# Strip network of the last stage: up products over 256 columns in place of two halves of 128

## Chip, cores and metric

The kernel runs on one core of a Trainium2 chip. The metric is the device time of the whole kernel in microseconds; less is better. The kernel before was run three times.

## What is computed

The input x has 16 sequences of 256 tokens and 256 features, float32. Four layers follow one another, each added to x: an attention layer, a gated cumulative layer, a mixture of experts with a shared network, and a recurrent network. Cut to the parts that the last stage of the kernel computes:

```python
# layer 3, the shared network of the mixture (256 -> 1024 -> 256)
shared = jax.nn.gelu(context_c @ sw1 + sb1, approximate=True) @ sw2 + sb2
return out + shared            # out: the routed experts

# layer 4, the recurrence
xw = jnp.einsum('ntd,dh->nth', x, Wx) + b
def step(prev_h, xw_t):
    next_h = jnp.tanh(xw_t + prev_h @ Wh)
    return (next_h, next_h)
_, hs = jax.lax.scan(step, h0, jnp.swapaxes(xw, 0, 1))
```

The recurrence has 256 steps that can only be done one after the other. The shared network has no such order, but its result for a token must be there before the recurrence reaches that token.

## The kernel before, in words

Three stages run one after the other: attention and the gated layer, the routed experts, and the last stage, `shared_and_rnn` (line 1635). Only the last one is touched. It begins at about 955 us of the span.

The last stage does the shared network and the recurrence at the same time. Tokens are taken in chunks of 16 (CH), so that a chunk has N = 16 sequences x 16 tokens = 256 columns; there are 16 chunks, and the first two were done by the stage before, so 14 are left. Features lie on the 128 partitions in two groups (DC = 2). The hidden 1024 of the shared network are FC = 8 blocks of 128.

*Strips.* Every product of this stage is cut into four matmuls whose results are 32 partitions high (QD = 4, QW = 32), one for each quarter of the output partitions; the helper `strips` (lines 1730 to 1734) issues the four for a product of the shared network. They use the array's column groups beside one another. A float32 matmul leaves two matmul and two weight-load records in the trace, so a strip product of four matmuls has 8 of each.

*Recurrence.* For each step k, `recur(k)` on TensorE (line 1711) multiplies the state with Wh: 8 matmuls of 64 columns (16 records, line 1716) into the PSUM tile `pr`. VectorE transposes the result (line 1813), ScalarE takes the tanh (line 1789), and the state is ready for step k+1. For each pair of steps, `drive` (line 1719) adds the input product with Wx (line 1727, 16 records) after an even step. VectorE puts the bias back after an odd step (line 1816).

*Shared network between the steps.* `ffn(c)` (line 1736) is a generator that yields after each strip product. For a block n of the hidden units of a chunk, it waits until the gelu has freed the PSUM tile (a ring of three) and issues the up products: two halves of the 256 columns, and for each half the two feature groups, so four strip products of 128 columns. The last one signals `up_ok`. ScalarE then takes the gelu of the whole 256 columns (line 1797) and signals `gelu_ok`. Two blocks later come the down products, two strip products of 256 columns, which sum over the eight blocks in `pys` and signal `down_ok`. When a chunk is complete, VectorE adds it to x (line 1827) for the recurrence, which needs the tile that POOL has staged for the output before (line 1859). POOL also joins the two parts of x into `xf` for the next chunks (line 1852) and waits for `up_ok` before it overwrites a tile.

*The order of the work* is written by hand. `order()` (line 1677) lists the strip products with a size in units, 1 for an up product of 128 columns and 2 for a down product of 256; `quota(k)` (line 1673) grants a step 4 units, or 3 in every fourth step from step 64 on:

```python
return 3 if k >= 4 * CH and k % 4 == 2 else 4
```

A loop (lines 1688 to 1695) turns this into `counts[k]`, the number of strip products that TensorE issues after the recurrence's own matmuls of step k, and into `ended`, the step in which a block ends. What is taken too much from one quota is missing in the next. From `ended` come the steps in which ScalarE has its gelus (after the tanh of that step, line 1794) and VectorE its adds (line 1837). With a quota of 4, a step holds for example four up products, or two down products, or two up and one down. The last down product falls into step 234; the remaining steps have only the recurrence.

Of the kernel before, what the change touches and what calls it, by code (L numbers as in the profile page):

```python
# [12 lines left out]
P = 128  # L13
B, T, D = 16, 256, 256
DC = D // P
# [1280 lines left out]
def experts(nc, env):  # L1296
# [9 lines left out]
    with st:  # L1306
# [24 lines left out]
        with ExitStack() as routed:  # L1331
# [225 lines left out]
            def _(pe):  # L1557
# [68 lines left out]
                for t in range(TICKS + 2):  # L1626
                    if t < TICKS:
                        up(t)
                    if t >= 2:
                        down(t - 2)  # L1630

        shared_and_rnn(nc, env, locals())


def shared_and_rnn(nc, env, ex):
# [4 lines left out]
    xhi, xlo, raw1, raw2, wx, wh = (ex[k] for k in ("xhi", "xlo", "raw1", "raw2", "wx_sb", "wh_sb"))  # L1640
    N = B * CH
    QD = 4
    QW = P // QD
    RING = 3
    PAIRS = T // 2
    HALF = N // 2
    KEEP = 4
    st = ExitStack()
    with st:  # L1649
# [6 lines left out]
        xf = sb(st, "xf", [P, 2, DC, B, CH])  # L1656
        ph = [ps(st, f"phs{q}", [P, 512]) for q in range(RING)]
# [7 lines left out]
        xf_ready, up_ok, gelu_ok, down_ok = (sem(st, n) for n in ("xf_ready", "up_ok", "gelu_ok", "down_ok"))  # L1665
# [3 lines left out]
        def quad(w, j):  # L1669

            return w.rearrange("p (k q) -> p k q", q=P)[:, :, QW * j:QW * (j + 1)]
# [5 lines left out]
        def order():  # L1677

            for c in range(FIRST, NCH):
                for n in range(FC + 2):  # L1680
                    if n < FC:
                        for a in range(2 * DC):
                            yield 1, (("up", c, n) if a == 2 * DC - 1 else None)
                    if n >= 2:
                        for m in range(DC):
                            yield 2, (("down", c, n - 2) if m == DC - 1 else None)

        counts, ended, left, item = [0] * T, {}, 0, order()
        for k in range(T):
            left += quota(k)  # L1690
# [17 lines left out]
        @block.tensor  # L1708
        def _(pe):
            def recur(k):  # L1710
                pe.wait_ge(h_ready, k + 1)
                prev = hs[:, (k - 1) // CH % 2, (k - 1) % CH]
                dst = steps[k // 2 % 2].rearrange("p (k q) -> p k q", q=QW)
                for c in range(DC):
                    for j in range(QD):
                        i = nc.tensor.matmul(dst[QW * j:QW * (j + 1)], prev[:, c], quad(wh[:, c], j), start=False, stop=(c == DC - 1), skip_group_check=True)  # L1716
                i.then_inc(step_done, 1)

            def drive(p):

                c, s, at = 2 * p // CH, 2 * p // CH % 2, 2 * p % CH
                pe.wait_ge(x_ready, c + 1)
                dst = steps[p % 2].rearrange("p (k q) -> p k q", q=QW)
                pe.wait_ge(bias_set, p + 1)
                for k in range(DC):
                    for j in range(QD):
                        nc.tensor.matmul(dst[QW * j:QW * (j + 1)], xc[:, s, k, at:at + 2].rearrange("p t b -> p (t b)"), quad(wx[:, k], j),  # L1727
                                         start=False, stop=False, skip_group_check=True)

            def strips(dst, weights, moving, start, stop):  # L1730

                for j in range(QD):
                    i = nc.tensor.matmul(dst[QW * j:QW * (j + 1)], weights[:, QW * j:QW * (j + 1)], moving, start=start, stop=stop)  # L1733
                return i

            def ffn(c):

                pe.wait_ge(xf_ready, c - FIRST + 1)
                for n in range(FC + 2):
                    if n < FC:  # L1740
                        pe.wait_ge(gelu_ok, FC * (c - FIRST) + n + 1)
                        for a in (0, HALF):
                            for k in range(DC):
                                moving = xf[:, c % 2, k].rearrange("p b t -> p (b t)")[:, a:a + HALF]
                                i = strips(ph[n % RING][:, a:a + HALF], raw1[:, k, n * P:(n + 1) * P], moving, k == 0, k == DC - 1)
                                if k == DC - 1 and a > 0:
                                    i.then_inc(up_ok, 1)
                                yield
                    if n >= 2:
                        f = n - 2  # L1750
                        pe.wait_ge(gelu_ok, FC * (c - FIRST) + f + RING + 1)
                        if f == 0 and c > FIRST:
                            pe.wait_ge(x_ready, c)
                        for m in range(DC):
                            i = strips(py[:, m, 0:N], raw2[:, f, m * P:(m + 1) * P], g[:, f % KEEP], f == 0, f == FC - 1)
                            if m == DC - 1:
                                i.then_inc(down_ok, 1)
                            yield

            def all_ffn():  # L1760
                for c in range(FIRST, NCH):
                    yield from ffn(c)

            pe.wait_ge(ex["wxh_in"], 32)
            work = all_ffn()
            pe.wait_ge(row1_set, 2)
            for half_pair in steps:
                dst = half_pair.rearrange("p (k q) -> p k q", q=QW)
                for j in range(QD):
                    i = nc.tensor.matmul(dst[QW * j:QW * (j + 1)], row1[:], quad(vec("rnn_b_row"), j), start=True, stop=True, skip_group_check=True)  # L1770
                i.then_inc(bias_rows, 1)
            drive(0)
            for k in range(T):
                recur(k)
                if k % 2 == 0 and k // 2 + 1 < PAIRS:
                    drive(k // 2 + 1)
                for _ in range(counts[k]):
                    next(work, None)
# [157 lines left out]
```

## Time and profile before

| what | us |
|---|---|
| median of 3 runs | 1312.1 |
| lowest, highest | 1312.03, 1315.19 |
| the profiled execution, its own time | 1311.1 |
| span of that execution, first to last instruction | 1309.3 |
| TensorE matmuls busy in the span | 1198.6 (92%) |
| TensorE weight loads busy in the span | 946.4 (72%) |
| VectorE, ScalarE, POOL busy | 805.0, 622.5, 335.7 |
| mean granted clock of TensorE | 0.973 of full |

Times of the trace count from the first instruction. PE stands for TensorE's matmuls, PEld for its weight loads (they overlap the matmuls), DVE for VectorE, ACT for ScalarE. Matmuls are pipelined and their ends are modelled: a record's duration is longer than the time until the next one can start, so many records of some 270 ns follow one another every 27 ns. "issue" as what an engine waited for means that the profile shows nothing that it waited for. Some matmul records can be missing.

### The profile page before, as it was taken

What the parts mean: (1) busy time and instruction counts of PE and PEld (TensorE: products, weight loads), DVE (VectorE), ACT (ScalarE), POOL (GpSimd) and SP (SyncE); (2) the same over time, 40 slices, a digit from 0 to 9 for tenths busy, and PEclk for the clock granted to TensorE, in tenths of its full rate; (3) what the DMA queues carried; (4) which work ended last, traced back from release to release, by engine and by line L of the source; (5) the groups of instructions that cost most, each with busy time, mean ns of one, the idle gap of its engine ahead of it and who ended that gap; (6) DMA issues with size and microseconds to landing.
All of it is one profiled execution on the core that took longest, in us unless ns stands there. A gap on an engine that the chain in (4) does not pass through costs nothing. (4 is left out here: it accounts for less than half of the span.)

```text
span 1309.3 us, 42133 instructions
## 1 busy us (share of the span) xinstructions
PE 1198.6 (92%) x18136; PEld 946.4 (72%) x18136; DVE 805.0 (61%) x1823; ACT 622.5 (48%) x1168; POOL 335.7 (26%) x311
## 2 busy tenths in 40 slices
PE   4699999999999888499999999999989989999995
PEld 2466666767665443159999999999977777777773
DVE  6887887878875979956666665666632332323322
ACT  2377777777767879333333333333323333333331
POOL 1446445544452679600000000000020101111100
PEclk9799999999999989799999999999999999999995
DMA  9013221212212100059999999999600000000000
GB/s 358 2 51 98 68 81 50 99 50 73 76 50 82 65 0 1 0 212 396 379 366 366 360 368 370 359 369 363 224 12 13 13 20 13 21 13 21 21 13 19
DMA packets 77096, 180.41 MB, mean 138 GB/s; under 512 B 3824, under 2 KB 14192, under 8 KB 76656
## 3 DMA queue, kind: packets, MB, share of 16 engines
q1 hardware_dynamic: 76912, 177.72, 37.6%
q8 instruction: 144, 2.36, 0.8%
q14 instruction: 40, 0.33, 0.1%
HBM read 156.47 MB, written 20.97 MB: 136 GB/s over the span
## 5 line engine op out<-in xcount | busy, mean ns | idle before, releaser
L1416 ACT ACTIVATE g<-ph,b 128x256 f32<-128x256 f32 x256 | 121.6, 475 | 247.9 <-PE ph L1605 247.8
L1813 DVE STREAM_TRANSPOSE preT<-pr 128x64 f32<-128x64 f32 x256 | 64.0, 250 | 234.7 <-PE pr L1716 234.0
L693 DVE TENSOR_REDUCE mx<-pR 128x4 f32<-128x1024 f32 x128 | 156.4, 1225 | 65.0 <-PE pR L899 63.6
L1525 DVE CAST ghi<-g 128x256 fp32r<-128x256 f32 x256 | 74.8, 292 | 128.2 <-ACT g L1416 128.0
L1733 PE MATMUL phs<-xf,raw 128*32 128x128 f32 x3584 | 144.0, 275 | 10.5 <-issue 10.4
L1789 ACT ACTIVATE hs<-preT 128x32 f32<-128x32 f32 x256 | 58.7, 229 | 197.7 <-DVE preT L1813 196.0
L1621 PE MATMUL py<-ghi,w 128*128 128x256 f32 x512 | 145.7, 285 | 1.7 <-DVE glo L1527 1.6
L1603 PE MATMUL ph<-xhi,w 128*128 128x256 f32 x512 | 145.3, 284 | 0.0
L1604 PE MATMUL ph<-xlo,w 128*128 128x256 f32 x512 | 144.9, 283 | 0.0
L1622 PE MATMUL py<-glo,w 128*128 128x256 f32 x512 | 144.9, 283 | 0.0
L1623 PE MATMUL py<-ghi,w 128*128 128x256 f32 x512 | 144.9, 283 | 0.0
L1605 PE MATMUL ph<-xhi,w 128*128 128x256 f32 x512 | 144.9, 283 | 0.0
L1716 PE MATMUL pr<-wh_sb,hs 128*32 128x64 f32 x4096 | 130.7, 228 | 15.0 <-ACT hs L1789 9.2
L1733 PE MATMUL pys<-gs,raw 128*32 128x256 f32 x1792 | 136.8, 380 | 2.4 <-issue 1.3
L490 ACT ACTIVATE raw<-pR 128x1024 f32<-128x1024 f32 x128 | 129.3, 1024 | 18.8 <-PE pR L908 17.2
L1716 PEld LDWEIGHTS pr<-wh_sb,hs 128*32 128x32 f32 x4096 | 99.8, 113 | 48.2 <-ACT hs L1789 34.2
L1733 PEld LDWEIGHTS phs<-xf,raw 128*32 128x32 f32 x3584 | 106.9, 111 | 19.4 <-issue 17.2
L1527 DVE TENSOR_TENSOR glo<-g,ghi 128x256 fp32r<-128x256 f32 x256 | 108.9, 426 | 8.8
L1842 POOL MEMSET row<- 128x32 f32 x1 | 0.1, 125 | 404.6 <-POOLq L1331 404.6
L1621 PEld LDWEIGHTS py<-ghi,w 128*128 128x128 f32 x512 | 98.2, 192 | 3.2 <-DVE glo L1527 3.1
L1604 PEld LDWEIGHTS ph<-xlo,w 128*128 128x128 f32 x512 | 98.3, 192 | 0.2 <-issue 0.2
L1603 PEld LDWEIGHTS ph<-xhi,w 128*128 128x128 f32 x512 | 98.3, 192 | 0.2 <-issue 0.2
(219 smaller groups left out, 2461.2 us busy)
## 6 DMA issues: line engine op xcount, KB each, us to landing
w<-weight_halves SPq DMA_DIRECT2D x128, 1024.0 KB, 8.0
weight_halves<-wparts SPq DMA_DIRECT2D x32, 512.0 KB, 4.0
modw<-in_ew SPq DMA_DIRECT2D x32, 256.0 KB, 4.7
xn<-in_x_tok SPq DMA_DIRECT2D x4, 1024.0 KB, 11.8
XT<-in_x_dm SPq DMA_DIRECT2D x2, 2048.0 KB, 14.4
out_dm<-staged SPq DMA_DIRECT2D x16, 256.0 KB, 2.4
raw<-in_sw SPq DMA_DIRECT2D x2, 1024.0 KB, 7.5
modw<-in_mod_w SPq DMA_DIRECT2D x1, 768.0 KB, 7.1
```

The costliest lines, as they stand in the source:

```text
L490: nc.scalar.activation(probs[:, j % 4], pR[k][:], ACT.Exp, scale=HD ** -0.5).then_inc(free[k], 1)
L693: nc.vector.reduce_max(mx[:, :, 2 * j:2 * j + 2].rearrange("p t s -> p s t"), pR[k][:].rearrange("p s (t k) -> p s t k", t=TC), AX.X).then ...
L1416: nc.scalar.activation(g[:, t % RING], ph[t % RING][:, 0:T], ACT.Gelu_apprx_tanh, bias=b1[:, n, f:f + 1]).then_inc(gelu_done, 1)
L1527: nc.vector.tensor_tensor(glo[:, t % RING], g[:, t % RING], ghi[:, t % RING].bitcast(fp32), ALU.subtract).then_inc(lo_done, 1)
L1603: nc.tensor.matmul(dst, whi, hi, start=(k == 0), stop=False)
L1604: nc.tensor.matmul(dst, whi, lo, start=False, stop=False)
L1605: i = nc.tensor.matmul(dst, wlo, hi, start=False, stop=(k == DC - 1))
L1621: nc.tensor.matmul(dst, whi, hi, start=(f == 0), stop=False)
L1622: nc.tensor.matmul(dst, whi, lo, start=False, stop=False)
L1623: i = nc.tensor.matmul(dst, wlo, hi, start=False, stop=(f == FC - 1))
L1716: i = nc.tensor.matmul(dst[QW * j:QW * (j + 1)], prev[:, c], quad(wh[:, c], j), start=False, stop=(c == DC - 1), skip_group_check=True)
L1733: i = nc.tensor.matmul(dst[QW * j:QW * (j + 1)], weights[:, QW * j:QW * (j + 1)], moving, start=start, stop=stop)
```

## The change

In `order()` an up product has the size 2, and there are two of them (one for each feature group) in place of four of size 1. In `ffn` the loop over the two halves is gone: each strip product streams all 256 columns, and the last of the two signals `up_ok`. Results, tiles, semaphores and their counts stay.

```diff
@@ -1643,7 +1643,6 @@
     QW = P // QD
     RING = 3
     PAIRS = T // 2
-    HALF = N // 2
     KEEP = 4
@@ -1679,8 +1678,8 @@
             for c in range(FIRST, NCH):
                 for n in range(FC + 2):
                     if n < FC:
-                        for a in range(2 * DC):
-                            yield 1, (("up", c, n) if a == 2 * DC - 1 else None)
+                        for k in range(DC):
+                            yield 2, (("up", c, n) if k == DC - 1 else None)
                     if n >= 2:
                         for m in range(DC):
                             yield 2, (("down", c, n - 2) if m == DC - 1 else None)
@@ -1739,13 +1738,11 @@
                 for n in range(FC + 2):
                     if n < FC:
                         pe.wait_ge(gelu_ok, FC * (c - FIRST) + n + 1)
-                        for a in (0, HALF):
-                            for k in range(DC):
-                                moving = xf[:, c % 2, k].rearrange("p b t -> p (b t)")[:, a:a + HALF]
-                                i = strips(ph[n % RING][:, a:a + HALF], raw1[:, k, n * P:(n + 1) * P], moving, k == 0, k == DC - 1)
-                                if k == DC - 1 and a > 0:
-                                    i.then_inc(up_ok, 1)
-                                yield
+                        for k in range(DC):
+                            i = strips(ph[n % RING][:, 0:N], raw1[:, k, n * P:(n + 1) * P], xf[:, c % 2, k], k == 0, k == DC - 1)
+                            if k == DC - 1:
+                                i.then_inc(up_ok, 1)
+                            yield
                     if n >= 2:
                         f = n - 2
                         pe.wait_ge(gelu_ok, FC * (c - FIRST) + f + RING + 1)
```

## Rows read from the trace of the kernel before

**Rows 1.** Windows of the last stage: length, each engine busy (instructions), clock, DMA share, GB/s

```profile
core 0: us, PE busy (x) PEld busy (x) DVE busy (x) ACT busy (x) POOL busy (x), PEclk, DMA share, GB/s
955.00:1279.80 324.80, 301.39 (x11056) 250.66 (x11056) 99.69 (x384) 104.56 (x348) 37.94 (x43) 0.99 0.05 16
1279.80:1304.10 24.30, 15.67 (x464) 11.27 (x464) 7.52 (x29) 4.35 (x19) 1.41 (x2) 0.57 0.04 13
```

**Rows 2.** Groups by shape, TensorE's matmuls, 955 to 1279.8 us

```profile
line engine op names shapes xcount | busy us, mean ns | idle before us <-releasers
L1733 PE MATMUL phs<-xf,raw 128*32 128x128 f32 x3584 | 144.0, 275 | 10.5 <-issue 10.4
L1733 PE MATMUL pys<-gs,raw 128*32 128x256 f32 x1792 | 136.8, 380 | 2.4 <-issue 1.3 <-ACT gs L1797 0.7
L1716 PE MATMUL pr<-wh_sb,hs 128*32 128x64 f32 x3776 | 118.3, 222 | 5.8 <-issue 4.8
L1727 PE MATMUL pr<-wx_sb,xc 128*32 128x64 f32 x1904 | 57.7, 221 | 4.8 <-issue 3.8 <-DVE pr L1809 0.8
```

**Rows 3.** Chain of work, 1098 to 1106 us: start, us, what

```profile
1099.11 0.44 PE phs L1733 x16
1099.55 0.43 PE pys L1733 x8
1099.98 0.22 PE pr L1716 x16
1100.20 0.22 PE pr L1727 x16
1100.43 0.43 PE pys L1733 x8
1100.86 0.71 issue
```

**Rows 4.** Waits, 955 to 1279.8 us: us in total, times, longest

```profile
engine line waited for: us in total, times, longest us
...
PEld phs L1733 <- issue: 17.2, 23, 1.2
...
PEld pr L1716 <- issue: 8.5, 20, 1.0
PEld pr L1727 <- issue: 5.9, 12, 1.0
PEld pys L1733 <- issue: 5.0, 10, 1.0
```

**Rows 5.** Windows between two pauses (two), and one without a pause; columns as in rows 1

```profile
1072.13:1076.12 3.99, 3.29 (x127) 2.93 (x127) 1.21 (x5) 1.45 (x5) 0.00 (x0) 1.00 0.02 4
1101.56:1105.40 3.84, 3.27 (x127) 2.56 (x128) 1.21 (x5) 1.09 (x4) 0.00 (x0) 1.00 0.02 4
1231.19:1234.38 3.19, 3.19 (x138) 2.94 (x130) 1.80 (x6) 1.39 (x5) 0.00 (x0) 1.00 0.02 5
```

**Rows 6.** Queue of instruction packets (packets, MB, share): 955 to 1279.8, then 1060 to 1105 us

```profile
q8 instruction: 87, 1.43, 1.9%
...
q8 instruction: 12, 0.20, 2.0%
```

**Rows 7.** VectorE in order of time, from two stretches

```profile
978.91 0.25 DVE L1813 STREAM_TRANSPOSE preT<-pr 128x64 f32<-128x64 f32 x1 [0.57 <-PE pr L1716]
979.94 0.61 DVE L1827 TENSOR_TENSOR xc<-XT,pys 128x256 f32<-128x256 f32 x1 [0.78 <-POOL staged L1859]
980.40 0.21 DVE L1813 STREAM_TRANSPOSE preT<-pr 128x64 f32<-128x64 f32 x1
...
1021.96 0.25 DVE L1813 STREAM_TRANSPOSE preT<-pr 128x64 f32<-128x64 f32 x1 [0.57 <-PE pr L1716]
1023.27 0.25 DVE L1813 STREAM_TRANSPOSE preT<-pr 128x64 f32<-128x64 f32 x1 [1.06 <-PE pr L1716]
...
1024.36 0.25 DVE L1813 STREAM_TRANSPOSE preT<-pr 128x64 f32<-128x64 f32 x1 [0.57 <-PE pr L1716]
```

**Rows 8.** All engines in order of time, 1126 to 1132 us

```profile
1127.99 0.43 PE L1716 MATMUL pr<-wh_sb,hs 128*32 128x64 f32 x16
...
1128.77 0.23 ACT L1789 ACTIVATE hs<-preT 128x32 f32<-128x32 f32 x1 [0.83 <-DVE preT L1813]
...
1129.21 0.64 PE L1733 MATMUL pys<-gs,raw 128*32 128x256 f32 x8
...
1129.48 0.47 ACT L1797 ACTIVATE gs<-phs,small 128x256 f32<-128x256 f32 x1 [0.48 <-PE phs L1733]
```

## Prediction

> **What bounds the kernel now.** I read first the windows of the last stage [rows 1]. Everything before 955 us is untouched by the edit. From 955.0 to 1279.8 us the recurrence and the strip network share TensorE; from there to the end only recurrence is left, at a lower clock. The first stretch is 324.8 us and the only one that can change. TensorE is busy in 301.4 of it, at a clock of 0.99 of full (the 2.4 GHz level). So the stretch looks bound by TensorE's work; the question is whether this busy time is columns or something that goes with the number of instructions.
>
> The groups by shape [rows 2] give the counts: 3584 matmul records of the up products (each float32 matmul leaves two records, each with its own weight load), 1792 of the down products, 3776 of the recurrence's state product and 1904 of its input product: 11056, and as many weight loads.
>
> Then the chain of waits of one stretch, which gives the price of a piece when nothing disturbs it [rows 3]: 16 records of up with 128 columns take 0.44 us, 8 records of down with 256 columns 0.43 us, a state product or an input product (16 records of 64 columns) 0.22 us. These are the same 27 ns per record of 128 columns, 54 ns per record of 256 and 14 ns per record of 64: **time follows columns, not instructions**. By this view alone the edit is worth nothing, since 8 records of 256 columns replace 16 of 128. But the last row of the group is 0.71 us of "issue": TensorE had work, all its operands, and did not start.
>
> The waits put down to issue [rows 4] are 65 pauses of the weight-load side, 36.6 us together. Where are they? I cut the stretch from the end of one such pause to the end of the next [rows 5]: 127 matmuls and 127 or 128 weight loads, in 3.99 and in 3.84 us. That is 256 instructions with a semaphore instruction or two, each time, whatever the instructions are. The DMA view shows what comes in such a rhythm [rows 6]: 12 instruction packets in 45 us, 87 in the stretch, 16 KB each by the queue's bytes, against 22112 / 256 = 86.4 blocks of 256 instructions. So TensorE's instructions are fetched one block at a time, and **when the engine has run through a block before the next has come, it stands**. The stretch averages 324.8 / 86.4 = 3.76 us a block. A fetch cycle costs at most 3.19 us where no pause is seen (last of rows 5, 268 instructions) and 3.84 to 3.99 us where one is. The engine wants blocks faster than that; it is bound by the supply of instructions.
>
> The Trainium skill speaks against this reading, and so against any gain: "Runtime: NRT & Kernel Launch", section "Instruction fetch mechanics", says that 16 KiB blocks are prefetched while the current one runs, and that the fetch is hidden because dispatch is slower than the fill. The block size agrees with the trace; "hidden" doesn't, by the 65 pauses. By that rule the sum would be 0.
>
> **The change, part by part.**
>
> *Columns:* 112 blocks of up products, each 4 x 0.22 us before and 2 x 0.43 us after [rows 3]. Difference nothing; the bound on it is the 0.44 against 0.43, at most 112 x 0.02 = 2 us of gain, and I take 0. The pace of weight loads is no new limit, for there are fewer.
>
> *Instructions:* 1792 matmul and 1792 weight-load records go. 22112 becomes 18528, 72.4 blocks in place of 86.4. At 3.76 us a block these would take 272 us, less than TensorE and the recurrence need when never short of instructions. So the bound moves, and the new stretch is worked out from the undisturbed pace.
>
> *The undisturbed pace:* transposes, one to a step, stand 1.31 us apart over a step with an input product and four units of strip work, and 1.09 us over one without [rows 7]. The first is columns: 0.22 + 0.22 + 2 x 0.43. The second is columns (1.08) and equally the round from state product over transpose and tanh. The hand-written quota, with items of 2 units only, gives 235 steps to the last down product, as before: 118 with an input product, of which 96 carry four units and 22 fewer (1.09 then, by the round), and 117 without. 96 x 1.31 + 139 x 1.09 = 277.3 us.
>
> *The quota's unevenness:* before, items of 1 unit allowed 3 units beside an input product and 5 in the next step; now it is 4 and 4, or 2 where the quota has 3 left over. 1.09 + 1.30 against 1.31 + 1.09: nothing. Ten steps go from 3 units to 2, for which fifteen others go from 3 to 4, all within TensorE's spare time; at most 10 x 0.2 = 2 us, already in the 277.3.
>
> *What stays beside it:* 1.2 us from 955.0 to the first transpose, about as much in the first step at the lower clock, and four adds on VectorE that wait for POOL, each stretching a step from 1.09 to 1.49 us [rows 7]. I estimate 4 us; unchanged.
>
> *Order of signals:* up_ok comes with the last of the up records, as before, and 22 of the 112 blocks now end one step earlier. Behind up_ok waits the gelu on ScalarE, and behind the gelu the tanh of the next step. The gelu starts 0.27 us after the instructions that follow its up products, takes 0.47, and the tanh is due 0.78 us after the state product [rows 8]: 0.04 us of room where the up block is last in its step. I cost it at nothing, hidden by that room; if it went, the next state product would be late.
>
> *Fetch stalls that are left:* two steps hold 160 instructions (32 state, 32 input, 96 strip) and take 2.40 us. 256 are that pair and 96 more, which take 1.31 us in four of five positions of the boundary and 1.96 in the fifth: 3.71 or 4.36 us. Against a cycle of 3.19 to 3.99 us the second never stalls. The first stalls a little: with a cycle around 3.75, give or take 0.2, about 0.1 us over 58 blocks, 5 to 6 us; I take 5. The ends are 0 and 0.28 x 58 = 16 us.
>
> Sum: 277.3 + 4 + 5 = 286.3 us in place of 324.8, so 38.5 less. The profiled execution took 1311.1 us, 1 us under the median: 1272.6 for it, **1273** for the median. As a check the same way of reckoning for before: 278 + 4 and the 36.6 us of pauses make 319, against 324.8; some pauses that look like waits for the tanh are missing in the count.
>
> The tail of 20 steps at half clock keeps its 24.3 us [rows 1]; DMA queues, SP and POOL have nothing moved.
>
> **Rivals.**
>
> *A fixed price per block.* If crossing a boundary cost the same whatever ran between, the 324.8 - 282 = 43 us over 86.4 blocks would be 0.5 us each, and 14 fewer give 7 us: 1305. Against it: one block ran in 3.19 us with no pause while others paused 0.7 us. 7%.
>
> *No gain.* If the pauses had another cause, one that goes with time and columns and not with the number of instructions, they would stay, and the time with them: 1312. Against it: the 256 instructions from pause to pause, and a fetch to each. 5%. The skill's rule of hidden fetches leads to this case too.
>
> *The gelu in front of the tanh, slower.* 256-column records end later after their start than those of 128 (380 against 275 ns, rows 2); if up_ok came late enough, each of the 112 gelus would push a tanh back by up to its own 0.47 us, 53 us: 1273 + 53 = 1326. It decides the sign only if the delay is over 38.5 / 112 = 0.34 us in each. Against it: the last of 8 wide records also starts earlier, and 0.04 us of room is there. A delay of 0.05 in each, 6 us, is in the range. 2%.
>
> *The change does something else* (the three-dimensional operand read more slowly, or split again into halves): the records of up would not halve; near 1312 or above. 2%.
>
> **How the numbers follow.** The fetch reading has 84%: 1273, with ends 1267 (no stall left) and 1284 (each block at 3.99 us), and 1290 if the gelus cost 6 us too. The two smallest effects that could lie beneath 1267 are 2 us of columns: 1265. The range 1265 to 1289 leaves out the rivals, 16%. A measurement of this kernel can tell about 0.3%, 4 us. Faster by more: 0.93 (the first case, the fixed price and some intermediate outcomes); within: 0.04; slower: 0.03.
>
> **What would show it.** Right: up records 1792 of 128x256 at about 380 ns; instruction packets in the stretch 73 in place of 87; the time put down to issue below 12 us in place of 36.6; transposes mostly 1.31 and 1.09 us apart; the stretch near 286 us and still 235 steps; tail unchanged. Wrong: pauses per block as long as now (fixed price), waits of tanh or of the state product in steps that end with an up block (gelu), pieces of 8 up records longer than 0.43 us in the chain (operand), or a cycle that is itself longer than 3.99 us.

## The result and the profile after

The changed kernel takes 1266.26 us (median; 1265.18 to 1268.35 in 4 runs) against 1312.92 us beside it: ratio 0.9644, 95% interval 0.9625 to 0.9663. That is 46.7 us faster; 1273 was forecast, within 1265 to 1289. Two executions at a far lower granted clock (1945.2 us for the kernel before beside e5 to e8, at 0.65 of full, and 1512.7 us for e8, at 0.77) are left out of the medians below.

The profiled execution has a span of 1263.3 us, 46.0 less than before. By the transposes on VectorE, one to a step, it splits so: the first stands at 953.87 us, 2.3 earlier than before, in code that the change doesn't touch (in the kernels below it lies anywhere from 953.4 to 958.2); the 234 steps up to the last down product take 278.9 us in place of 322.1; the 21 steps of the tail 25.7 in place of 26.1. So **43.2 us come from the shared stretch**, where 38.5 were forecast.

The windows of the same two parts of the stage, and the groups by shape of the first, in the changed kernel (lines are 1 lower at TensorE and 3 lower elsewhere than before):

```profile
core 0: us, PE busy (x) PEld busy (x) DVE busy (x) ACT busy (x) POOL busy (x), PEclk, DMA share, GB/s
952.70:1234.30 281.60, 280.97 (x9264) 195.31 (x9264) 99.77 (x384) 105.21 (x348) 37.94 (x43) 0.99 0.05 17
1234.30:1258.20 23.90, 15.03 (x464) 10.77 (x464) 7.55 (x30) 4.36 (x20) 1.42 (x2) 0.60 0.04 14
```

```profile
line engine op names shapes xcount | busy us, mean ns | idle before us <-releasers
L1732 PE MATMUL phs<-xf,raw 128*32 128x256 f32 x1792 | 127.3, 381 | 0.0
L1732 PE MATMUL pys<-gs,raw 128*32 128x256 f32 x1792 | 126.6, 379 | 0.0
L1715 PE MATMUL pr<-wh_sb,hs 128*32 128x64 f32 x3776 | 100.8, 220 | 0.0
L1726 PE MATMUL pr<-wx_sb,xc 128*32 128x64 f32 x1904 | 51.3, 221 | 0.8 <-DVE pr L1806 0.8
```

Against [rows 1] the stretch has 9264 matmul records in place of 11056 and takes 281.6 us in place of 324.8. Against [rows 2] the down products, which nobody changed, are busy 126.6 us in place of 136.8, and the state products 100.8 in place of 118.3: the same work, in groups that no pause cuts in two any more. The waits put down to issue, pauses on the weight-load side in which nothing that the profile shows was waited for, tell it directly. These rows answer to [rows 4]:

```profile
engine line waited for: us in total, times, longest us
...
PEld pys L1732 <- issue: 0.7, 3, 0.3
PEld pr L1715 <- issue: 0.4, 2, 0.2
PEld phs L1732 <- issue: 0.4, 2, 0.2
PEld pr L1726 <- issue: 0.2, 1, 0.2
```

8 pauses of 1.7 us together in place of 65 of 36.6. That is 34.9 us less, and the stretch is 43.2 shorter. The other 8.3 us are split by no view. One pause of 0.9 us before is put down to the gelu; and a pause is not the whole delay, for in the chain of before the 16 up records behind the pause at 1100.86 take 0.65 us in place of 0.44. How much that makes in all was not measured. The queue of instruction packets over the stretch has 73 in place of 87 [rows 6], as worked out from 18528 / 256:

```profile
q8 instruction: 73, 1.20, 1.9%
```

The chain of work (start, us, what), which answers to [rows 3], is columns from end to end in the window shown: the two up products of a block (16 records) take the same 0.86 us as two down products.

```profile
1090.98 0.22 PE pr L1715 x16
1091.20 0.22 PE pr L1726 x16
1091.42 0.86 PE pys L1732 x16
1092.29 0.22 PE pr L1715 x16
1092.51 0.86 PE phs L1732 x16
1093.38 0.22 PE pr L1715 x16
```

### The profile page after: what moved, and what is told of

The parts are those of the page before. It is cut to its first block and busy times, and to the rows that moved or that the text cites. A ratio compares the mean times of both kernels' runs of the same rounds, so it can differ in the third digit from the quotient of the medians.

```text
span 1263.3 us, 38549 instructions
## 1 busy us (share of the span) xinstructions
PE 1175.9 (93%) x16344; PEld 889.6 (70%) x16344; DVE 805.4 (64%) x1823; ACT 622.6 (49%) x1168; POOL 335.7 (27%) x311
## 5 line engine op out<-in xcount | busy, mean ns | idle before, releaser
L1715 PEld LDWEIGHTS pr<-wh_sb,hs 128*32 128x32 f32 x4096 | 88.2, 113 | 66.4 <-ACT hs L1786 51.8
L1732 PE MATMUL phs<-xf,raw 128*32 128x256 f32 x1792 | 127.3, 381 | 0.0
L1732 PE MATMUL pys<-gs,raw 128*32 128x256 f32 x1792 | 126.6, 379 | 0.0
L1715 PE MATMUL pr<-wh_sb,hs 128*32 128x64 f32 x4096 | 112.7, 226 | 9.4 <-ACT hs L1786 9.4
L1603 PEld LDWEIGHTS ph<-xhi,w 128*128 128x128 f32 x512 | 98.3, 192 | 0.2 <-issue 0.2
L1605 PEld LDWEIGHTS ph<-xhi,w 128*128 128x128 f32 x512 | 98.3, 192 | 0.0
```

The source lines that it names most:

```text
L1603: nc.tensor.matmul(dst, whi, hi, start=(k == 0), stop=False)
L1605: i = nc.tensor.matmul(dst, wlo, hi, start=False, stop=(k == DC - 1))
```

## Experiments

**Is it the number of instructions, or the order, or something of the up products?** Four kernels ran on one chip, with the kernel before at 1312.86 us beside them.

e1 keeps the halves and takes the new order of work ("..." marks lines left out):

```diff
-                        for a in range(2 * DC):
-                            yield 1, (("up", c, n) if a == 2 * DC - 1 else None)
+                        for a in range(2):
+                            yield 2, (("up", c, n) if a == 1 else None)
...
                                 if k == DC - 1 and a > 0:
                                     i.then_inc(up_ok, 1)
-                                yield
+                            yield
```

> The kernel before, its up products still in halves of 128 columns, but given out in the new order: an item of two units is one half with both feature groups, so that every step carries the strip work that it carries in the changed kernel. TensorE's instructions stay 22112 in the stretch. Theory (supply of instructions, one block of 256 in about 3.75 us): no gain, 1312, within 4 us. Rival (the gain comes from the order, that is from 4 and 4 units in place of 3 and 5): 1266. Rival (the order costs and the merging hid it): over 1316.

Measured: 1312.28 us, ratio 1.0011 (0.9993 to 1.0029). Order gives nothing and costs nothing within the interval (1 us less to 4 us more); both rivals fall.

e2 takes the changed kernel and cuts the down products instead (only the first half carries the start flag, only the second the stop flag; the last argument is new in `strips`, which passes it on as `skip_group_check`):

```diff
...
-                            i = strips(py[:, m, 0:N], raw2[:, f, m * P:(m + 1) * P], g[:, f % KEEP], f == 0, f == FC - 1)
+                            for a in (0, N // 2):
+                                i = strips(py[:, m, a:a + N // 2], raw2[:, f, m * P:(m + 1) * P], g[:, f % KEEP, a:a + N // 2],
+                                           f == 0 and a == 0, f == FC - 1 and a > 0, True)
```

> The changed kernel with its down products, not its up products, cut into two halves of 128 columns: 3584 narrow records of down, 1792 wide ones of up, again 22112 instructions in the stretch. Theory (supply): the stalls are back, about 1312, and 87 instruction packets in the stretch. Rival (something of the up products alone, such as up_ok, the gelu or the PSUM ring, had been slow in halves): 1266 to 1270.

Measured: 1314.57 us, ratio 1.001 (0.9995 to 1.0025), 87 instruction packets in the stretch. The waits of that stretch are back, now with the down products in front, and the whole gain of the change is gone while its up products are as the change made them:

```profile
PEld pys L1732 <- issue: 14.5, 24, 1.3
PEld pr L1726 <- issue: 10.5, 13, 1.5
PEld pr L1715 <- issue: 10.0, 20, 1.1
PEld phs L1732 <- issue: 9.0, 16, 1.2
```

e3 is e1 with e2's edit, so both up and down are in halves.

> Both up and down in halves, in the new order: 3584 + 3584 narrow records, 25696 instructions in the stretch, 100.4 blocks. Theory (supply): a cycle of 3.75 to 3.85 us a block gives a stretch of 376 to 387 us, so 1361 to 1371. Rival (a fixed price of 0.5 us at each block boundary on top of the undisturbed 282): 1266 + 50 = 1316. Rival (up products alone): 1312.

Measured: 1367.69 us (1365.04 to 1370.33), ratio 1.0416 (1.038 to 1.0453). The window of its stretch and its instruction packets:

```profile
955.00:1338.50 383.50, 306.07 (x12848) 280.21 (x12848) 100.24 (x386) 105.64 (x347) 38.30 (x44) 1.00 0.04 14
```

```profile
q8 instruction: 101, 1.65, 1.9%
```

The windows of the stretch in e1 and in e2:

```profile
957.00:1287.00 330.00, 302.19 (x11056) 248.37 (x11056) 99.92 (x384) 105.65 (x348) 37.96 (x43) 0.99 0.05 16
956.60:1284.70 328.10, 300.48 (x11056) 251.44 (x11056) 100.24 (x384) 105.45 (x348) 37.78 (x43) 0.99 0.05 16
```

e3 has 25696 instructions, 100.4 blocks of 256, 3.82 us each. For e1 it is 330.0 / 86.4 = 3.82, for e2 328.1 / 86.4 = 3.80, for the kernel before 3.76. (The profiled executions of e1, e2 and e3 took 5.6, 1.6 and 2.6 us more than their medians; less that, it is 3.76, 3.78 and 3.79.) Over a range of some 55 us in time the price of a block stays within 2%, where a fixed price of 0.5 us at each boundary would have given 1316.

Two more readings of e3's trace show that a pause belongs to a block and to a fetch. Its 98 pauses put down to issue make 97.8 us, and from each to the next lie 126, 127 or 128 weight loads and as many matmuls, in all 97 cases. And 95 of the 98 end 2.1 to 2.9 us after the start of an instruction packet. **The stretch takes the number of blocks times one fetch cycle, once that is more than its columns take.**

e4 keeps the halves and the old order but does an up product as one matmul over all 128 output partitions, which takes instructions away without touching the halves:

```diff
-                                i = strips(ph[n % RING][:, a:a + HALF], raw1[:, k, n * P:(n + 1) * P], moving, k == 0, k == DC - 1)
+                                i = nc.tensor.matmul(ph[n % RING][:, a:a + HALF], raw1[:, k, n * P:(n + 1) * P], moving, start=k == 0, stop=k == DC - 1)
```

> The kernel before with its halves and its own order, but each half of an up product is one matmul over all 128 output partitions in place of four strips of 32: 1792 fewer matmul calls, 16736 instructions in the stretch, 65.4 blocks. Theory (supply): if such a matmul of 128 columns takes no more time than the four strips together (0.22 us), no stall is left and the time is 1266, although the halves are there. Rival (halves of 128 columns cost by themselves): about 1312. Unknown: the price of weight loads of 128 columns and of the change between strips and the whole array; more than 0.1 us for each of 448 products would bring it to 1312 as well, and the chain would show it as longer pieces, not as pauses.

Measured: 1319.37 us, ratio 1.0054 (1.0034 to 1.0073). By its time alone this would speak for the rival. The window of its stretch and the chain show what was named as unknown:

```profile
954.60:1287.50 332.90, 332.71 (x8368) 249.49 (x8368) 99.72 (x382) 105.50 (x347) 37.81 (x43) 1.00 0.04 14
```

```profile
1094.32 0.86 PE phs L1745 x6
1095.18 0.36 PE pr L1716 x16
1095.54 1.09 PE phs L1745 x8
1096.63 0.36 PE pr L1716 x16
1096.99 0.22 PE pr L1727 x16
1097.21 1.09 PE phs L1745 x8
```

TensorE's matmul side stands still for 0.2 us in the whole stretch, so halves alone make no pauses. But in the chain four halves over the whole array take 1.09 us in place of 0.87, and the state product behind them 0.36 in place of 0.22. That is 0.36 us for a step of four up units, and uses up the whole gain. Most of it goes with the change between strips and whole array: by their starts in the trace, whole-array records follow one another every 0.112 us, 0.90 us for eight, hardly more than the strips' 0.87; only the second comes 0.21 us after the first. So about 0.2 us are paid going in (an estimate) and 0.14 coming out. The verdict rests on the window and the chain, not on the time.

**Is the changed kernel free of the limit, or just past it?** Four more kernels, beside 1313.8 us.

e5 and e6 make the quota exact. A planner cuts a product where the step ends in its middle:

```diff
-            left += quota(k)
+            left = quota(k)
...
+                if left == 1:
+                    split.append(True)
+                    left, rest = 0, (what,)
...
+                halves = ((0, N // 2), (N // 2, N)) if next(parts) else ((0, N),)
+                for a, z in halves:
+                    i = strips(dst[:, a:z], weights, moving[:, a:z], start and a == 0, stop and z == N)
```

and e6 has `return 3 if k > 4 * CH and k % 8 in (0, 6) else 4` as its quota.

> The changed kernel with an exact quota: the steps k % 4 == 2 from 64 on carry exactly 3 units, in place of 4 and 2 by turns, so that none of them leaves TensorE idle. Where a step's end cuts a strip product of two units, the product is done as two halves: 84 of 448 are. By columns the steps would take 5.3 us less than in the changed kernel. But the 84 halves bring back 1344 instructions: 688 for 8 steps, which would take 9.14 us undisturbed. Theory (supply): 688 / 256 = 2.69 blocks at 3.6 to 3.75 us are 9.7 to 10.1 us, in place of the 9.37 of the changed kernel, over some 21 such groups: 7 to 15 us more, 1273 to 1281. Rival (columns and the round of the recurrence alone): 1261.

> The same with the two light steps of eight put next to one another (k % 8 in 6 and 0 after step 64), so that only 42 products are cut: 656 instructions in 8 steps, 2.56 blocks. Theory (supply): at 3.6 to 3.75 us a block 9.2 to 9.6 us, against 9.14 by columns and 9.37 in the changed kernel: 1262 to 1271, between the changed kernel and e5. Rival (columns): 1261.

Measured: e5 1282.77 us (ratio 0.9764, 0.9736 to 0.9793), e6 1272.97 us (0.9707, 0.9681 to 0.9733). The same columns, spread so that the steps should take 5 us less, and yet 16.5 and 6.7 us slower than the changed kernel: **84 cut products cost 16.5 us, 42 cost 6.7**. These medians come from two jobs; the traces agree, with 17.1 and 6.8 us more for the 234 steps, and with 41 pauses put down to issue of 18.3 us in e5 and 32 of 10.2 in e6, against 8 of 1.7. The rival's 1261 is excluded by both. The theory's own ranges end 2 us too low for both. A likely reason, not tried: the blocks of these kernels are uneven, and a slow block lends nothing to a fast one, so that an average over groups of eight steps understates. The window of e5's stretch, 19872 instructions in 77.6 blocks of 3.85 us:

```profile
953.40:1252.00 298.60, 288.67 (x9936) 228.46 (x9936) 99.69 (x383) 104.40 (x348) 37.95 (x43) 0.99 0.05 17
```

e7 halves the number of instructions of the shared network, with strips of 64:

```diff
-                for j in range(QD):
-                    i = nc.tensor.matmul(dst[QW * j:QW * (j + 1)], weights[:, QW * j:QW * (j + 1)], moving, start=start, stop=stop)
+                for j in range(2):
+                    i = nc.tensor.matmul(dst[64 * j:64 * (j + 1)], weights[:, 64 * j:64 * (j + 1)], moving, start=start, stop=stop)
```

e8 is e5 with the same edit.

> The changed kernel with the strip products of the shared network done as two matmuls of 64 output partitions in place of four of 32: 3584 instructions fewer (14944 in the stretch, 58.4 blocks). Theory: the supply no longer binds in the changed kernel, so fewer instructions give at most the 1 us of pauses that are left: 1265 to 1266, if two strips of 64 stream as fast as four of 32. Rival (TensorE is still bound by the number of its instructions): a seventh less, up to 10 us, 1256. Unknown: a change of strip height before each state product, which e4 showed to cost 0.14 us (0.36 in place of 0.22) from the whole array: at that price 1266 + 235 * 0.14 = 1299.

> e5's exact quota with e7's strips of 64. If e7 comes out at 1266, supply is no longer short, and the halves are free: 1261, 5 us under the changed kernel and 12 to 20 under e5, at the same quota and the same columns. If e7 pays for the strip height, this pays the same, less 5 us. Rival (halves are slow whatever the supply): e7 plus 7 us or more.

Measured: e7 1327.81 us (ratio 1.0116, 1.0098 to 1.0134), e8 1327.3 us (1.0115, 1.0092 to 1.0139). The 1299 that I had named for a price on the state product alone was too low. The chain of e7:

```profile
1092.53 0.36 PE pr L1715 x16
1092.89 0.22 PE pr L1726 x16
1093.11 0.58 PE phs L1732 x4
1093.70 0.36 PE pr L1715 x16
1094.06 1.01 PE pys L1732 x8
1095.07 0.36 PE pr L1715 x16
```

The change of strip height costs 0.14 to 0.15 us in both directions: 0.36 in place of 0.22 for the state product, and 0.58 in place of 0.43 (or 1.01 in place of 0.86) for what follows the recurrence's own matmuls. Over 235 steps 0.29 us each would be 68 us; 61 were measured in the stretch, since a light step has room for some of it. So e7 can't say whether fewer instructions would help the changed kernel. The pair says something else: e5's 84 cut products, which cost 16.5 us at strips of 32, cost nothing measurable at strips of 64 (1327.3 against 1327.81), where the supply is not short: TensorE is busy in 342.1 of 342.8 us of e7's stretch and in 342.6 of 343.3 of e8's. The 5 us that e8 was to gain aren't there. The reason follows from the pieces: with the added 0.29 us even a light step is bound by TensorE and leaves nothing idle that an exact quota could fill.

**Does the limit act block by block?** e10 has wide up products in even chunks and halves in odd ones, in `order()` as well as in `ffn`. It, e9 and the changed kernel once more (e11) ran in one job, beside 1311.25 us.

```diff
...
+                        W = N if c % 2 == 0 else HALF
+                        for a in range(0, N, W):
```

> Up products of 256 columns in even chunks, halves in odd ones: half of the instructions that the change takes away, 20320 in the stretch, 79.4 blocks. Theory (supply): the merged chunks run at the pace of the changed kernel, 18.7 to 19.4 us for 16 steps, the others at that of before, 21 to 22.5 us, alternating in one trace; 1287 to 1291 in all. Rival (a slower pace that builds up or a state that the whole stage is in): no alternation.

Measured: 1290.13 us (1287.64 to 1292.61, two runs), ratio 0.9833. Windows over the steps of chunks 3, 4, 5 (16, 16 and 16 steps):

```profile
core 0: us, PE busy (x) PEld busy (x) DVE busy (x) ACT busy (x) POOL busy (x), PEclk, DMA share, GB/s
976.76:999.66 22.90, 20.64 (x784) 16.85 (x774) 6.75 (x26) 7.46 (x24) 2.66 (x4) 1.00 0.05 16
999.66:1018.96 19.30, 19.30 (x656) 13.24 (x649) 6.75 (x27) 7.45 (x24) 2.68 (x4) 1.00 0.05 18
1018.96:1041.31 22.35, 20.42 (x780) 16.96 (x769) 6.74 (x26) 7.46 (x24) 2.68 (x4) 1.00 0.05 16
```

ScalarE and VectorE do the same in each row. With halves 1558 instructions take 22.90 us and TensorE stands 2.26; without, 1305 take 19.30 and it never stands. The pace changes with the chunk and goes back, so it is no state of the stage. The first of the three is 0.4 us slower than the 22.5 that was expected at most.

**The tail.** e9 is the changed kernel with its idle tail filled:

```diff
-                for _ in range(counts[k]):
-                    next(work, None)
+                if k < ended["down", NCH - 1, FC - 1] + 1:
+                    for _ in range(counts[k]):
+                        next(work, None)
+                elif k < T - 1:
+                    if k == ended["down", NCH - 1, FC - 1] + 1:
+                        pe.wait_ge(gelu_ok, FC * (NCH - FIRST) + RING)
+                    for _ in range(1 + k % 2):
+                        strips(ph[k % RING][:, 0:N], raw1[:, 0, 0:P], xf[:, 1, 0], True, True)
```

> The changed kernel, and in the tail after the last down product, where TensorE has only the recurrence and its granted clock falls to the lower level, one strip product of 256 columns in each even step and two in each odd one, whose result nobody reads. The tail of the changed kernel takes 25.7 us for 21 steps, most of them 1.29 us apart, against 1.06 to 1.09 at the higher clock. Theory: work that fits into the round of the recurrence keeps the clock up: 21 steps at 1.06 to 1.10 are 22.5 to 23.5 us, so 2 to 3 us less than the changed kernel in the same job, 1263 to 1264. Rival (the extra work delays the state products): the tail stays at 25 us or grows, 1266 to 1270.

> The changed kernel itself, for the comparison with e9 on the same chip: 1266, within 2 us.

Measured: e9 1264.1 us (1261.49 to 1266.26 in 5 runs; ratio 0.9635, 0.9617 to 0.9653) against 1266.64 us (1264.72 to 1267.36 in 5 runs; ratio 0.9651, 0.9636 to 0.9667) for the changed kernel beside it. The intervals overlap, so the medians alone don't settle 2.5 us; the trace does for its part. The tail of e9:

```profile
1234.30:1255.50 21.20, 20.96 (x700) 12.13 (x692) 7.76 (x30) 4.58 (x20) 1.42 (x2) 1.00 0.05 17
```

The granted clock stays at 1.00, the 2.4 GHz level, where the changed kernel has 0.60 on average, and by the transposes the last 21 steps take 22.6 us in place of 25.7. The added products lie in the room that the round of the recurrence leaves: steps are 1.06 and 1.09 us apart.

## Why the prediction was right, step by step

*What bounds it:* right. The pauses were the bound, every 256 instructions; they went when instructions went (1.7 us left of 36.6), came back when other products were cut (e2), and grew when instructions grew (e3). One remark of the prediction doesn't hold: its check for the kernel before missed 5.8 us, which it put down to pauses that look like waits for the tanh. No wait of the state product for the tanh is over 0.5 us there, and the longest in the changed kernel is as long; where the 5.8 us lie stays open.

*The Trainium skill's rule against it:* "Runtime: NRT & Kernel Launch", section "Instruction fetch mechanics", holds the fetch for hidden. By that rule the result would have been 1312; e2 and e3 measure the opposite for a TensorE that has columns and operands ready for 22112 instructions in 282 us, 78 in a microsecond. In the changed kernel, at 66, the trace agrees with the rule.

*Columns:* right at zero. 0.86 us for four units in either width.

*Instructions:* right. 9264 records and as many weight loads, 73 packets.

*Undisturbed pace:* right, and 1.4 us too high. Of steps with an input product the median is 1.31 us, of those without 1.09. The 277.3 us and 4 us beside them make 281.3, and with the 1.7 us of pauses 283.0; the stretch took 281.6. By the transposes the 21 light steps take 1.06 us in place of 1.09, 0.6 us in all, and the four adds on VectorE that wait for POOL stretch the stage by some 0.7 us in place of 1.6.

*Quota:* right at nothing, by e1.

*Order of signals:* right at nothing. By the loop that makes the order, 73 of the 112 up blocks are now the last work of their step (51 before). The steps that end so have the same medians as the others: 1.31 us with an input product and four units, 1.09 without. The room of 0.04 us on ScalarE was enough.

*Stalls that are left:* **the term that was mis-sized.** I took 5 us, between 0 and 16; at most 1.7 are there. (The 160 instructions of two steps are 64 of state products, 32 of the input product and 64 of strips, not 32, 32 and 96; their sum, and what was worked out from it, stands.) I had put the fetch cycle at 3.75 give or take 0.2, from blocks that showed a pause. But a pause shows only where the cycle was long, or the block short, so those rows can't speak for the others; the prediction's own row of 3.19 us without a pause [rows 5] already lay far below them. In the changed kernel a window from one block's end to the next shows 131 weight loads and no idle matmul time in 3.64 us:

```profile
1050.96:1054.60 3.64, 3.64 (x140) 2.52 (x131) 1.98 (x6) 1.16 (x4) 2.32 (x3) 1.00 0.21 77
```

The cycle was thus no longer than that here, while the blocks of e1 to e3 averaged 3.80 to 3.82 us. It also varies while the engine is starved all the time: the instruction packets of e3 start 3.29 to 4.82 us apart. Whether it is shorter besides when the engine has not just been starved was not tried.

*Outside the sum:* 2.3 us of the span lie before the stage and are the earlier stages' own variation; the tail gave 0.4. The 46 us of the span are 43.2 + 2.3 + 0.4. Of the 4.7 us that the stretch gave beyond the 38.5 forecast, the stalls explain 3.3 (5 less 1.7) and the pace and what stands beside it the other 1.4.

*Rivals:* the fixed price falls by e3; no gain falls by the result; the slower one, the gelu in front of the tanh, never appeared.

## What to carry to other kernels

When an engine shows idle time put down to nothing, count the instructions from pause to pause. If the number is always the same (256 here) and an instruction packet goes with each, the kernel is bound by the supply of instructions: then price a change by instructions / 256 times the cycle (3.8 us here), compare that with what columns and dependencies need, and take the larger, chunk by chunk and not over the whole: e10's 79.4 blocks would take 302 us at 3.8, and its stretch took 307, since its wide chunks are bound by their columns. Past the point where the two meet, every small matmul brought back for a better balance is paid for again (e5, e6), so merge first and balance with what is left.

## What the runs showed of the hardware

A change of strip height on TensorE costs time: 0.14 us from the whole array to strips of 32 and about 0.2 the other way in e4, and 0.14 to 0.15 both ways between 64 and 32 in e7, where it makes 61 us. Apart from that change, matmuls of 128 columns over the whole array follow one another every 0.112 us in e4, where four strips take 0.11. And the lower clock in the tail can be bought off with work of no use (e9): 21 steps in 22.6 us in place of 25.7.
